# An adaLN block with an oscillator scan and a channel mixer: ScalarE's read-outs and VectorE's work reordered in the even slots

## The reference, cut to what matters

```python
h = layernorm(x) * (1 + ca) + sa
# first half: a damped oscillator for each of 64 modes, scanned over the 2048 rows
omega = clip(softplus(h @ W_omega.T + b_omega), 1e-4, 100);  zeta = sigmoid(h @ W_zeta.T + b_zeta)
A = omega**2;  S = 1 / (1 + DT*DT*A);  d = 1 - zeta;  F = h @ W_B.T + b_B
z_new = d * (S*z - DT*A*S*y) + F_z;  y_new = d * (DT*S*z + S*y) + F_y      # row after row
x = x + ga * (states @ C.T + h @ D_mat.T)
# second half: channel mixing with the row before
h = layernorm(x) * (1 + cb) + sb
xr = mu_r*h + (1-mu_r)*h_prev;  xk = mu_k*h + (1-mu_k)*h_prev
x = x + gb * sigmoid(xr @ W_r.T) * (relu(xk @ W_k.T)**2 @ W_v.T)
```

## Time and profile before

| what | value |
|---|---|
| median of 3 runs | 998.7 us |
| the profiled execution's own time | 1001.2 us |
| its span | 999.4 us |
| granted TensorE clock, mean share of full speed | 0.982 |
| TensorE busy | 942.6 us (94%) |
| VectorE busy | 819.8 us (82%) |
| ScalarE busy | 700.2 us (70%) |
| GpSimd busy | 91.8 us (9%) |

### The profile page before, as it was taken

How to read it: one execution, slowest core, us unless ns; L and a number is a source line. 1 busy time by engine, 2 the same in 40 slices (tenths; PEclk the granted TensorE clock), 3 DMA queues, 4 the chain that set the end, 5 groups by cost and what they waited for, 6 DMA issues and landing times.

```text
span 999.4 us, 14767 instructions
## 1 busy us (share of the span) xinstructions
PE 942.6 (94%) x5019; PEld 787.6 (79%) x5020; DVE 819.8 (82%) x2270; ACT 700.2 (70%) x1371; POOL 91.8 (9%) x117
## 2 busy tenths in 40 slices
PE   8977959899999999999999999999999999998997
PEld 3556848788888878887888878788887878887886
DVE  4878769897979979797988979798997979797563
ACT  4979767668777686777767676876768687755451
POOL 0001001000100102010000201000020102010000
PEclk9999988899999999999999999999999999999899
DMA  9720301020211302021131302121120201111001
GB/s 329 271 69 1 106 21 64 24 89 16 85 53 44 95 27 89 13 85 43 43 95 43 95 1 88 40 70 58 44 95 22 94 23 43 43 43 43 22 22 43
DMA packets 35275, 64.78 MB, mean 65 GB/s; under 512 B 3704, under 2 KB 4344, under 8 KB 35200
## 3 DMA queue, kind: packets, MB, share of 16 engines
q1 hardware_dynamic: 35200, 63.84, 19.2%
HBM read 47.02 MB, written 16.81 MB: 64 GB/s over the span
## 4 chain that ended last, share of the span: by engine, by line
DVE 43%; PE 24%; ACT 17%; issue 10%; POOL 4%; DMA 1%; SPq 0%; DVEq 0%; ACTq 0%; POOLq 0%
PE ps_kr L328 8%; DVE mix_full L979 6%; PE ps_cd L328 6%; PE ps_tv L328 5%; POOL var L1467 3%; DVE bn_parts L1017 3%; DVE rt L1042 3%; DVE rt L1033 2%; DVE x L998 2%; DVE x L1049 2%; DVE xn L1006 2%; DVE tmp L1200 2%; DVE h_lo L910 2%; DVE tmp L1124 2%; DVE xn L993 1%
## 5 line engine op out<-in xcount | busy, mean ns | idle before, releaser
L979 DVE SCALAR_TENSOR_TENSOR mix_full<-ps_tv,cur_m,mix_full 128x256 f32<-128x256 f32 x256 | 117.6, 477 | 25.3 <-ACT mix_full L725 25.2
L747 ACT ACTIVATE kk<-ps_kr 128x512 f32<-128x512 f32 x64 | 38.1, 597 | 136.4 <-PE ps_kr L328 136.4
L725 ACT ACTIVATE mix_full<-ps_tv,cur_m 128x255 f32<-128x255 f32 x256 | 119.8, 574 | 14.4 <-PE ps_tv L369 14.3
L1467 POOL TENSOR_SCALAR var<-sq 128x2 f32<-128x2 f32 (+1 forms) x35 | 40.0, 1142 | 700.2 <-ACT square_out L584 700.2
L328 PE MATMUL ps_kr<-mix_k_hi,wk_hi 128*128 128x256 f32 x512 | 80.7, 280 | 5.3 <-issue 5.3
L328 PE MATMUL ps_kr<-mix_k_lo,wk_hi 128*128 128x256 f32 x512 | 80.0, 279 | 0.0
L328 PE MATMUL ps_kr<-mix_k_hi,wk_lo 128*128 128x256 f32 x512 | 79.8, 278 | 0.0
L328 PEld LDWEIGHTS ps_kr<-mix_k_hi,wk_hi 128*128 128x128 f32 x512 | 70.9, 190 | 8.4 <-issue 5.9
L328 PE MATMUL ps_tv<-wv_hi,kk_hi 128*128 128x512 f32 x256 | 72.8, 408 | 0.8 <-issue 0.8
L328 PE MATMUL ps_kr<-wr_hi,mix_r_hi 128*128 128x512 f32 x256 | 70.5, 397 | 2.2 <-ACT kk L747 2.2
L328 PE MATMUL ps_tv<-wv_lo,kk_hi 128*128 128x512 f32 x256 | 70.2, 397 | 0.0
(11 more groups left out here) (215 smaller groups left out, 2240.2 us busy)
## 6 DMA issues: line engine op xcount, KB each, us to landing
x<-in_x SPq DMA_DIRECT2D x32, 512.0 KB, 3.8
out<-x SPq DMA_DIRECT2D x32, 512.0 KB, 2.8
x_in<-in_x SPq DMA_DIRECT2D x15, 1024.0 KB, 5.2
x<-in_wmod SPq DMA_DIRECT2D x3, 1024.0 KB, 8.0
mix_full<-in_wmod SPq DMA_DIRECT2D x2, 1024.0 KB, 9.1
x_in<-in_x SPq DMA_DIRECT2D x2, 512.0 KB, 5.7
stage_out<-in_wd SPq DMA_DIRECT2D x1, 1024.0 KB, 10.3
stage_mix<-in_wmod SPq DMA_DIRECT2D x1, 1024.0 KB, 10.7
```

The source lines that it names most:

```text
L725: mm = act.activation(mix[n][:, k, 1:UNIT], ps_tv[:, j, c * UNIT:(c + 1) * UNIT - 1], ACT.Identity, bias=cur_m[:, SHIFT + k:SHIFT + k + 1] ...
L747: act.activation(kk[:, i, :], ps_kr[:, i, :], ACT.Relu).then_inc(s_relu, 1)
L979: dve.scalar_tensor_tensor(mix[n][:, k, :], ps_tv[:, j, c * UNIT:(c + 1) * UNIT], cur_m[:, alpha + k:alpha + k + 1], mix[n][:, k, :], ALU. ...
L1467: pool.tensor_scalar(var[:, :], sq[:, :], 1.0 / D, EPS, ALU.mult, ALU.add).then_inc(s_var, 1)
```

## The change

Only the even slots of the steady loop change, on two engines; the products, the loads and the odd slots keep their order. On ScalarE `states_out(q + 1)` and `tanh(u)` and `mix_high(u + 1, 1)` come ahead of `projections_out(q + 2)`, and `statistics2(u + 2)` comes ahead of `normalise1(q + 3)`. On VectorE `gated_tanh(u)` and the low parts of the mix come first, then step 1 of the recurrence, the residual, steps 2 and 3, the first tile of the read-out, steps 4 and 5, the second tile, and then normalise2 and the rest. No instruction is added or removed.

```diff
--- before.py
+++ after.py
@@ -872,21 +872,19 @@
                     relu_squared(u)
                     if next_mix:
                         mix_high(u + 1, 0)
-                    if q + 2 < NCHUNK:
-                        projections_out(q + 2)
                     if next_cd:
                         states_out(q + 1)
                     tanh(u)
                     if next_mix:
                         mix_high(u + 1, 1)
                     if q + 2 < NCHUNK:
+                        projections_out(q + 2)
                         softplus_parts(q + 2)
-                    if q + 2 < NCHUNK:
                         squared_angle(q + 2)
+                    if next_cd:
+                        statistics2(u + 2)
                     if next_t1:
                         normalise1(q + 3)
-                    if next_cd:
-                        statistics2(u + 2)
                 else:
                     relu_squared(u)
                     if next_mix:
@@ -1423,17 +1421,20 @@
                         run(mix_low(u + 1, 0))
                     if next_cd:
                         run(states_low(q + 1))
-                    take(rec, 1)
+                    run(gated_tanh(u))
                     if next_mix:
                         run(mix_low(u + 1, 1))
-                    take(rec, 2)
-                    run(gated_tanh(u))
+                    take(rec, 1)
                     if next_cd:
                         run(residual(u + 2))
-                        take(rec, 3)
-                    beside(rec, read_out(u), 2)
+                    take(rec, 2)
+                    out_of_banks = read_out(u)
+                    take(out_of_banks, 1)
+                    take(rec, 2)
+                    run(out_of_banks)
                     if next_cd:
                         beside(rec, normalise2(u + 2), 1)
+                    take(rec, 4)
                 else:
                     if s // 2 + 3 == CPB and next_t1:
                         new_columns(b + 1, tab_h, cur_h, s_cur_h)
```

## The result

The changed kernel takes 980.5 us (median of 4 runs, 980.22 to 981.75) against 998.85 us of the kernel before (997.58 to 999.46): ratio 0.9814, 95% interval 0.9802 to 0.9826. It is 18.35 us faster. The profiled execution took 980.24 us; its first to last instruction are 978.4 us apart, where before they were 999.4 us apart.

A forecast was written before the change was run, and what follows sets the result against it. VectorE's loop was taken to set the 57.76 us pair, TensorE's floor being 55.75. Waits of 8.3 + 6.9 us, plus 9 x 0.16 and 11 x 0.17, make 18.5 us off the 998.7 median: 980.2 us, range 977 to 989.5.

The forecast's parts named there:

- The sum: TensorE's waits for `xs_lo` and `xn` in the steady pairs, with the losses around them, go: 18.5 us.
- VectorE's new order: In the even slot VectorE idles 3.5 us in place of 6.4 and comes out 2.9 us earlier.
- The margin: Per steady pair, VectorE's loop of 54.9 us lies 0.9 us under TensorE's floor of 55.75 us.
- rival (1): VectorE keeps the lead: some 1.9 us more waits per pair, gain 1 us in eleven pairs, 987.7 us; chance 0.15.
- LN1's normalise at nothing: ScalarE's LN1 normalise (2.92 us), put last in the even slot, costs nothing; cover of 2 us before `shifted`.
- Rival (2): Late states delay ScalarE's tanh and reads, VectorE's step 1 and residual in every pair: 1012 us; chance 0.05.
- Rival (3): Port shared with VectorE stretches GpSimd's even-slot instruction from 0.19 to 3.64 us: 1006 us; chance 0.04.
- Rival (4): The waits only move, from the states to the odd slot: 998.7 us within 2 us; chance 0.05.
- What stays: First pair: ScalarE's 4.04 us wait for the scan's last step stays, and TensorE's stall there with it.

The follow-up runs named there:

- step1_behind_residual: Changed kernel with step 1 of the recurrence moved behind the residual on VectorE; 981.4 us, ratio 0.9828 to the kernel before.
- extra_2: Changed kernel plus two VectorE bn_stats instructions, read by nothing, in every even slot between recurrence steps 4 and 5; 981.95 us, ratio 0.9823.
- extra_4: Changed kernel plus four VectorE bn_stats instructions, read by nothing, in every even slot between recurrence steps 4 and 5; 992.04 us, ratio 0.9925.
- scalar_only: Kernel before with only the change's ScalarE order, VectorE keeping its old order; 1007.44 us, ratio 1.009.
- the two-input load: Changed kernel plus four unread two-SBUF-input VectorE tensor_tensor per even slot, 994.0 us; with a fifth of half width ahead of them, 1003.03 us.
- the scan edits: Changed kernel with recurrence steps taken earlier in the first pair and the last even slot, 968.9 us; in the first pair alone, 975.01 us.
- before_scan_earlier: Kernel before with recurrence steps taken earlier in the first pair and the last even slot; 988.31 us, ratio 0.9869.

## Why the prediction was right

**The sum.** 18.5 us were forecast and 18.35 measured. Both waits of the earlier trace rows went, for the reasons given: `xs_lo` is ready at 567.48 + 0.69 = 568.17, 3.6 us before TensorE takes up the states (3.4 forecast), and `xn` stands behind an rstd that no longer waits for LN1's normalise. The pair is 55.65 us for a forecast of 55.75, and `step1_behind_residual` shows TensorE as the bound.

It is luck that forecast and measurement are only 0.15 us apart. The sum was read from one profiled execution, and between the two profiled executions 1001.2 - 980.24 = 20.96 us went. The first and the last of these r products of TensorE have eleven steady pairs between them, in the kernel before and in the changed one:

```profile
227.96 1.08 PE L328 MATMUL ps_kr<-wr_hi,mix_r_hi 128*128 128x512 f32 x4
860.38 1.08 PE L328 MATMUL ps_kr<-wr_hi,mix_r_hi 128*128 128x512 f32 x4
```

```profile
226.89 1.08 PE L328 MATMUL ps_kr<-wr_hi,mix_r_hi 128*128 128x512 f32 x4
839.08 1.08 PE L328 MATMUL ps_kr<-wr_hi,mix_r_hi 128*128 128x512 f32 x4
```

They took 632.42 us and take 612.19 us: 20.2 us less, where the sum had 18.5, so the sum was some 1.7 us too small for the execution that it was read from. Against this, that execution lay 2.35 us above its kernel's median and the changed kernel's 0.26 us below, and the forecast took the sum from the median.

**VectorE's new order.** Steps and waits came as worked out: 2.94 us at step 1 in the pair shown and 3.2 in the mean for a forecast of 3.4, the read-out covering `hh`, no wait for rstd in the even slot (0.1 forecast).

**The margin was mis-sized.** "Under TensorE's 55.75 by 0.9 us" is the one term of VectorE's loop that missed: the room is 1.7 us by `extra_2` and `extra_4`, and the wait for `mix_full` in the changed kernel's odd slots is about as long (1.6 us). The forecast let VectorE idle 3.4 + 0.1 us in the even slot and 0.87 us in the odd one. It idles 3.2 us at step 1 (35.1 us in 11), not at all for rstd in the even slot, and 0.6 us in the odd one (7.0 us over eleven pairs), where `var` is not always the long one. That is 0.5 of the 0.8 us, and behind a long `var`, as in the pair that the forecast took, `extra_4` has 1.3 us of room in place of 0.9. The rest was not traced. VectorE's arrival at the odd slot's mixes, 598.6 us in the forecast, is at 586.88 - 1.44 = 585.44, in the old pair's time 585.44 + 11.89 = 597.3, 1.3 us earlier. Its input was there when forecast (586.88 + 11.89 = 598.8 for 598.7). Three parts of the 1.3 us are seen: ScalarE begins the states 0.47 us earlier (564.62 + 11.89 = 576.51 for 576.98), the 0.1 us for rstd is not spent, and one step of the recurrence, since the even slot issues 11 for 12, now comes behind the first mix where it stood ahead of it. It took 0.46 us there (601.07 to 601.53), in the kernel before:

```profile
601.07 0.55 DVE L1124 TENSOR_TENSOR tmp<-tree 128x384 f32<-128x384 f32 x1
```

This step moves the arrival and not the length of the loop. Too small a margin cost the prediction nothing but chance on rival (1), VectorE keeping the lead.

**LN1's normalise at nothing.** It holds, with 3 us of cover for the 2 that were counted: it ends at 581.83 us and `mix_full` starts at 584.84.

**Rival (2), late states.** The mechanism is real, and it happens in two pairs, not in all. In the first pair ScalarE waits 8.51 us for 4.04. In the last pair with projections, of which the forecast said nothing, it waits 4.55 us where before it did not wait:

```profile
844.87 0.42 ACT L700 ACTIVATE xs<-state 64x256 f32<-64x256 f32 x1 [4.55 <-DVE state L1221]
```

In the changed kernel VectorE's room takes both, and TensorE has no stall that it had not before. In `scalar_only`, where there is none, step 1 of the first pair comes 6.2 us later and the last pair with projections is 4.4 us longer; less the 1.2 us that the other pairs gain, these are about the 9 us lost. **Rival (3), the port,** needed a 3.64 us `var` in the even slot; it was 0.19 in all. Even the two-input load stretched the two instructions by less than 0.9 us. **Rival (4)** is out by the waits.

**What stays.** The first pair's stall (3.95 us, before 3.89) and the one at u = 28 (4.24 us, before 3.94) stayed, and went with the scan edits.

## What to carry to other kernels

When two engines hand work to each other in a loop, cost both orders together: either half of this change alone was slower than no change, and both were 1.8% faster. A wait that the new order adds is harmless as long as it is shorter than the waits it replaces and another engine sets the pace; load the engine with useless work of known length to read how much room it has, and look at the single pairs, since the mean can hide two kinds of them. And once the steady loop runs at its floor, look at its first and last turns, where two stalls of 4 us, with the lower clock around them, were worth 1.2%.

## What was unexpected in the hardware

GpSimd's `var` of two elements per partition takes one of a few lengths in the odd slots of the changed kernel (the first 12): 0.38 us in three pairs, 1.6 in two, 2.4 in one and 3.65 in six, beside the same row of VectorE instructions. Where it is 1.63 us, the next one, `rstd`, takes 2.47 for its usual 0.70:

```profile
597.33 1.63 POOL L1468 TENSOR_SCALAR var<-sq 128x2 f32<-128x2 f32 x1 [17.27 <-ACT square_out L584]
599.04 2.47 POOL L1470 TENSOR_TENSOR rstd<-var,minus_half 128x2 f32<-128x2 f32 x1
```

At 3.65 us it spans four and more of VectorE's instructions, so there it did not get in at the first boundary, as it did beside the added instructions of the even slot. Why is open.

In the kernel before the length of the pair goes with it. From one step 1 to the next, from 239 to 815 us, its eight pairs with a long `var` last 57.6 to 57.8 us; the two with a short one, which begin at 470 and at 642 us, last 57.0 and 56.8. (The ninth long `var` is in the last pair with projections, which has less work at its end and lasts 54.6 us.) In these two VectorE does not wait for rstd (nine waits in eleven pairs), and at the states that follow TensorE waits for `xs_lo` 0.24 us and not at all, for 0.9 to 1.1 us behind a long one. The short one of the pair at 470 us:

```profile
496.99 0.32 POOL L1467 TENSOR_SCALAR var<-sq 128x2 f32<-128x2 f32 x1 [16.30 <-ACT square_out L584]
```

By this comparison some 0.8 us in each of eight pairs, 6 to 7 of the 18 us gained, were waits behind GpSimd's small instruction. The changed kernel has these waits still (7.0 us of VectorE), but VectorE's room hides them. `before_scan_earlier`, whose steady pairs have the order of the kernel before, has another count and the same two lengths: of its eleven pairs from 177 to 807 us, five have the long `var` and last 57.6 to 57.8 us, and six have a short one and last 56.7 to 57.1 us. Whether the kernel before would be that much faster without the stretch was not tried.
